# One kernel, three attentions: scores as 32x64 products in two halves, the x transposes between them, and the context groups of the gate stage ahead of the x groups

## The reference

```
x = x + tanh(g_xattn[0]) * cross_attention(layernorm(x), ctx, ctx)      # 16 heads of 8
x = x + tanh(g_ffn[0])   * two_transformer_layers(layernorm(x))         # below
x = x + tanh(g_xattn[1]) * mlstm_attention(layernorm(x), ctx, ctx)      # 8 heads of 16, gates
x = x + tanh(g_ffn[1])   * int8_linear(layernorm(x))
# each transformer layer, l = 0, 1:
for l in range(L):
    x = x + _attn(_ln(x, ln1_w[l], ln1_b[l]), wq[l], wk[l], wv[l], wo[l], ...)   # causal, 16 heads of 8
    h = _ln(x, ln2_w[l], ln2_b[l])
    x = x + moe(h, ...)                  # 8 experts, top 2; by token for l = 0, by sequence for l = 1
# the heart of each attention:
att = jnp.einsum('bhqd,bhkd->bhqk', q, k) * hd ** (-0.5)
att = jax.nn.softmax(jnp.where(causal, att, -jnp.inf), axis=-1)
y = jnp.einsum('bhqk,bhkd->bhqd', att, v)
```

## Time and profile before

| what | value |
|---|---|
| three runs | 1271.04, 1274.37, 1277.46 us, median 1274.37 |
| the profiled execution | 1265.2 us, its span 1263.5 us |
| TensorE (PE) busy | 980.7 us, 78% |
| VectorE (DVE) busy | 836.2 us, 66% |
| ScalarE (ACT) busy | 700.8 us, 55% |
| GpSimd (POOL) busy | 584.5 us, 46% |
| masked keys, L632 | 192 instructions, 240.9 us |
| scores, 64x512 | 768 records, 103.4 us |
| chain that ended last | PE 48%, DVE 12%, ACT 9%, POOL 7% |

### The profile page before, as it was taken

One profiled execution on the slowest core, in us unless ns is written; L12 is line 12 of the kernel. 1 busy time (PEld: TensorE's weight loads), 2 busy tenths in 40 slices (PEclk: granted clock), 3 DMA queues, 4 the chain that ended last, 5 costly groups with the idle time before them and its releaser, 6 DMA issues.

```text
span 1263.5 us, 30781 instructions
## 1 busy us (share of the span) xinstructions
PE 980.7 (78%) x9835; PEld 759.3 (60%) x9835; DVE 836.2 (66%) x1984; ACT 700.8 (55%) x1780; POOL 584.5 (46%) x804
## 2 busy tenths in 40 slices
PE   4999998999974899993005999965999978899503
PEld 2677676677674799993003777744777758555301
DVE  4599998999848566661425999976222245389874
ACT  2577677878730177772004777743555522588643
POOL 6355544655620255554773666612333310378423
PEclk9899999999965599997556999966999995699855
DMA  4000040000020022221214000000000001011102
GB/s 124 12 13 15 15 137 2 2 0 0 1 67 0 17 67 64 65 65 47 53 52 134 2 0 0 1 2 0 0 0 0 0 25 50 7 47 44 30 0 67
DMA packets 51918, 38.74 MB, mean 31 GB/s; under 512 B 6072, under 2 KB 45476, under 8 KB 51860
## 3 DMA queue, kind: packets, MB, share of 16 engines
q1 hardware_dynamic: 46956, 28.88, 7.8%
q0 software_dynamic: 4320, 8.86, 2.7%
q10 hardware_dynamic: 584, 0.26, 0.1%
HBM read 29.13 MB, written 8.85 MB: 30 GB/s over the span
## 4 chain that ended last, share of the span: by engine, by line
PE 48%; DVE 12%; issue 11%; ACT 9%; POOL 7%; POOLq 7%; DVEq 3%; DMA 2%; SPq 1%; ACTq 0%
PE ps_s L1000 9%; PE ps_o L1000 8%; PE ps_t L1084 7%; PE ps_v L1000 6%; PE ps_a L1000 5%; PE ps_t L1000 5%; POOLq L688 5%; POOL h_all L659 2%; POOL w L659 2%; ACT work L811 2%; POOL work L689 2%; DVEq L1599 2%; PE ps_v L1104 1%; POOLq L678 1%; PE ps_x L1039 1%
## 5 line engine op out<-in xcount | busy, mean ns | idle before, releaser
L632 POOL TENSOR_TENSOR kbd<-kts,kmask 128x512 f32<-128x512 f32 x192 | 240.9, 1276 | 223.1 <-ACT qts L797 140.8
L652 POOL DMA_INDIRECT xg<-x_rows,row_from x71 | 73.5, 1036 | 137.8 <-DVE slot_of L1592 70.1
L819 ACT COPY probs_t<-ps_t 128x1024 f32<-128x1024 f32 x96 | 97.2, 1012 | 68.4 <-PE ps_t L1084 68.4
L1427 DVE TENSOR_REDUCE rowmax<-ps_s 128x16 f32<-128x1024 f32 x96 | 116.5, 1213 | 17.0 <-PE ps_s L1000 16.9
L1000 PE MATMUL ps_s<-kbd,qts 64*64 64x512 f32 (+1 forms) x1024 | 124.6, 559 | 0.2 <-issue 0.2
L1430 DVE TENSOR_TENSOR work<-ps_s,rowmax 128x1024 f32<-128x1024 f32 x96 | 117.6, 1225 | 3.3
L1000 PE MATMUL ps_o<-vst,probs_t 128*64 128x18 f32 x3072 | 108.5, 214 | 5.3 <-ACT probs_t L819 5.3
L1000 PEld LDWEIGHTS ps_o<-vst,probs_t 128*64 128x64 f32 x3072 | 98.9, 139 | 17.6 <-ACT probs_t L819 6.9
L1039 PE MATMUL ps_x<-ident,xn 128*128 128x128 f32 x96 | 31.1, 323 | 100.8 <-DVE xn L1418 100.8
L1084 PE MATMUL ps_t<-ident,work 128*128 128x128 f32 x768 | 103.5, 279 | 7.2 <-ACT work L811 5.7
L811 ACT ACTIVATE work<-work 128x1024 f32<-128x1024 f32 x96 | 100.9, 1051 | 1.3 <-DVE work L1430 1.2
(11 more groups left out here) (370 smaller groups left out, 2382.2 us busy)
## 6 DMA issues: line engine op xcount, KB each, us to landing
y_rows<-work SPq DMA_DIRECT2D x71, 64.0 KB, 1.6
w<-in_L_ffn_e_w_dram SPq DMA_DIRECT2D x2, 2048.0 KB, 8.6
ctx_dup<-in_ctx_dram SPq DMA_DIRECT2D x64, 64.0 KB, 2.3
x_res<-in_x_dram SPq DMA_DIRECT2D x4, 512.0 KB, 6.6
ctx_in<-in_ctx_dram SPq DMA_DIRECT2D x32, 64.0 KB, 1.8
x_rows<-h_all SPq DMA_DIRECT2D x1, 2048.0 KB, 9.2
work<-in_ctx_dram SPq DMA_DIRECT2D x8, 256.0 KB, 2.7
out_dram<-work SPq DMA_DIRECT2D x16, 128.0 KB, 1.8
```

Source lines behind the costliest of these rows:

```text
L632: i = pool.tensor_tensor(km[:, par, g, :, :], kts[:, par, g:g + 1, :].to_broadcast([P, 8, SEQ]), kmask[:, :, :], ALU.mult)
L652: pool.indirect_dma_start(xg[:, t % XBUFS, :], None, x_d, bass.IndirectOffsetOnAxis(row_from[:, t:t + 1], 0)).then_inc(xg_loaded[t % XBUFS ...
L819: nc.scalar.copy(probs_t[:, par, :], ps_t[:, :]).then_inc(S["pts_ready"], 1)
L1427: V.tensor_reduce(rowmax[:, par, :], s3, AXX, ALU.max).then_inc(S["max_ready"], 1)
```

## The change

- The head mask `kmask` covers 4 heads (`HPG`) in place of 8, and repeats every 32 partitions. GpSimd makes the masked keys of both sequences in one instruction of half the elements.
- The scores of a tile are eight products in place of four, each over 32 partitions (4 heads) and 256 columns: a 32x64 part of the array. They are issued in two halves. In the first, groups 0, 1, 2, 3 of heads belong to sequences 0, 1, 0, 1; in the second, to 1, 0, 1, 0. Different rows of the array would write the same bank and partitions if the halves overlapped, so the second waits for the first (`half_scored`).
- TensorE's transposes of context and x stand between the halves, in place of after the v projection; they wait for ScalarE's copy of the tile before.
- The causal mask is two products of 64x128 parts (`ident_seqs` stacks an identity for each sequence), in place of four of 64x64.
- VectorE's `norm_step` has lag 0 in place of 1 and stands last in the turn.
- In the gate stage all 8 context groups, their copies and their gate products come before the first x group, on TensorE and on ScalarE; there `row_std` stands after the context copies.

```
+GROUPS = 4
+HPG = HEADS // GROUPS
...
-                    for g in range(SPT):
-                        i = pool.tensor_tensor(km[:, par, g, :, :],
-                                               kts[:, par, g:g + 1, :].to_broadcast([P, 8, SEQ]),
-                                               kmask[:, :, :], ALU.mult)
-                    i.then_inc(S["kbd_ready"], 1)
+                    pool.tensor_tensor(km[:, par, :, :, :],
+                                       kts[:, par, :, :].unsqueeze(2).to_broadcast([P, SPT, HPG, SEQ]),
+                                       kmask[:, :, :].unsqueeze(1).to_broadcast([P, SPT, HPG, SEQ]), ALU.mult
+                                       ).then_inc(S["kbd_ready"], 1)
...
-            row_std(CH_MLSTM)
             for g in range(NB):
                 act.wait_ge(S["cg_tr"], g + 1)
                 nc.scalar.copy(inner[:, g * BLK:(g + 1) * BLK], (ps_o, ps_v)[g % 2][:, :]).then_inc(S["cg_sb"], 1)
+            row_std(CH_MLSTM)
+            for g in range(NB):
                 act.wait_ge(S["xg_tr"], g + 1)
...
+            def score_products(t, par, turned, masked):
+                for u in range(GROUPS):
+                    q, r, at = (u + turned) % SPT, u // 2, u % 2 * HPG * SEQ
+                    h_ = slice(32 * u, 32 * u + 32)
+                    yield mm(ps_s3[64 * q:64 * q + 64, r, at:at + HPG * SEQ], qts[h_, par, q * SEQ:(q + 1) * SEQ],
+                             km[h_, par, q, :, :].rearrange("p h k -> p (h k)"), not masked, True)
...
-                    for s in range(SPT if masked else 0):
-                        for r in range(2):
-                            h_ = slice(64 * r, 64 * r + 64)
-                            mm(ps_s3[64 * s:64 * s + 64, r, :], identb[h_, h_],
-                               causal[h_, :, :].rearrange("p a b -> p (a b)"), True, False)
-                    for s in range(SPT):
-                        for r in range(2):
-                            h_ = slice(64 * r, 64 * r + 64)
-                            i = mm(ps_s3[64 * s:64 * s + 64, r, :], qts[h_, par, s * SEQ:(s + 1) * SEQ],
-                                   km[h_, par, s, :, :].rearrange("p h k -> p (h k)"), not masked, True)
+                    for r in range(2 if masked else 0):
+                        h_ = slice(64 * r, 64 * r + 64)
+                        mm(ps_s3[:, r, :], ident_seqs[h_, :, :].rearrange("p s q -> p (s q)"),
+                           causal[h_, :, :].rearrange("p a b -> p (a b)"), True, False)
+                    for i in score_products(t, par, 0, masked):
+                        i.then_inc(S["half_scored"], 1)
+                return fn
+
+            def other_scores(base, masked):
+                def fn(t, par):
+                    pe.wait_ge(S["half_scored"], GROUPS * (ATT[base] + t + 1))
+                    pe.sem_inc(S["scores_begun"], 1)
+                    for i in score_products(t, par, 1, masked):
+                        pass
                     i.then_inc(S["scores_ready"], 1)
...
                 return [(L_SCORES, scores(base, l is not None)),
+                        (1, ctx_transpose(base)) if l is None else None, (1, transposes(base, nbase)),
+                        (L_SCORES, other_scores(base, l is not None)),
                         (L_OUT, transpose_y(base)), (L_WEIGH, transpose_probs(base)),
-                        (2, project(base, l)), (1, ctx_transpose(base)) if l is None else None,
-                        (1, transposes(base, nbase)), (L_OUT, out_project(base, l)), (L_WEIGH, weigh(base), VBUFS)]
+                        (2, project(base, l)), (L_OUT, out_project(base, l)), (L_WEIGH, weigh(base), VBUFS)]
...
             for g in range(NB + 1):
                 if g < NB:
                     context_group(g)
+                if g:
+                    context_gates(g - 1)
+            for g in range(NB + 1):
+                if g < NB:
                     x_group(g)
                 if g:
-                    i = gates_group(g - 1)
+                    i = x_gates(g - 1)
...
-                return [(L_OUT, y_step(base)), (1, norm_step(src, nbase, base, norm)),
-                        (L_SCORES, shift_step(base)), (L_OUT + 1, sums_step(dst, "x_updated", UPD[base])),
-                        (L_OUT, add_step(base, dst, scale))]
+                return [(L_OUT, y_step(base)), (L_SCORES, shift_step(base)),
+                        (L_OUT + 1, sums_step(dst, "x_updated", UPD[base])), (L_OUT, add_step(base, dst, scale)),
+                        (0, norm_step(src, nbase, base, norm))]
```

More of the change, by code:

```diff
@@ L194, in build @@
         identb = sb("identb", [P, P], BF16)
+        ident_seqs = sb("ident_seqs", [P, SPT, SEQ], BF16)
         ones_row = sb("ones_row", [1, P])
@@ L197, in build @@
         ones_b = sb("ones_b", [P, P], BF16)
-        kmask = sb("kmask", [P, 8, SEQ])
+        kmask = sb("kmask", [P, HPG, SEQ])
         kmask4 = sb("kmask4", [P, 4, SEQ])
@@ L234, in build @@
         kts = sb("kts", [P, 2, SPT, SEQ])
-        kbd = sb("kbd", [P, 2, 8, P])
-        km = kbd[:, :, :, :].rearrange("p b a n -> p b (a n)").rearrange("p b (s h k) -> p b s h k", s=SPT, h=8)
+        kbd = sb("kbd", [P, 2, HPG, P])
+        km = kbd[:, :, :, :].rearrange("p b a n -> p b (a n)").rearrange("p b (s h k) -> p b s h k", s=SPT, h=HPG)
         vst = sb("vst", [P, VBUFS, SPT, HEADS // 2, 2, HD + 1])
@@ L250, in build @@
         ctx4 = work[:, 2 * BLK:4 * BLK].rearrange("p (b a d) -> p b a d", b=2, a=SUB)
-        km16 = kbd[:, :, 0:4, :].rearrange("p b a n -> p b (a n)").rearrange("p b (s h k) -> p b s h k", s=SPT, h=4)
+        km16 = kbd[:, :, :, :].rearrange("p b a n -> p b (a n)").rearrange("p b (s h k) -> p b s h k", s=SPT, h=4)
         txs = work[:, 6 * DFF:6 * DFF + 2 * TURN].rearrange("p (b n) -> p b n", b=2)
@@ L559, in _ @@
             CONSTS.append(n[0])
-            head_mask(kmask, KM_HEADS, HD, SEQ, KM_HEADS * HD)
+            head_mask(kmask, HPG, HD, SEQ, HPG * HD)
             def routing_constants():
@@ L564, in routing_constants @@
                 select(identb[:, :], [[-1, P]], 0, 1, ALU.not_equal, 1.0)
+                fresh(pool.memset(ident_seqs[:, :, :], 0.0))
+                for half in range(2):
+                    part = ident_seqs[half * 64:(half + 1) * 64, :, :]
+                    select(part, [[0, SPT], [-1, SEQ]], 0, 1, ALU.not_equal, 1.0)
                 fresh(pool.memset(causal[:, :, :], 0.0))
@@ L1027, in fn @@
                 def fn(t, par):
+                    seen(pe, S["xts_ready"], TB[base] + t)
                     pe.wait_ge(ctx_loaded[par], arrived(t, par, 16))
@@ L1038, in fn @@
                     pe.wait_ge(S["xn_ready"], nbase + t + 1)
+                    if base != "x":
+                        pe.wait_ge(S["xts_ready"], TB[base] + t)
                     nc.tensor.transpose(ps_x[:, 0:P], xn[:, par, :], ident[:, :]).then_inc(S["xt_ready"], 1)
@@ L1264, in x_group, with context_gates, x_gates @@
                 i.then_inc(S["xg_tr"], 1)
-            def gates_group(g):
+            def context_gates(g):
                 pe.wait_ge(S["cg_sb"], g + 1)
+                for t in range(g * SUB, (g + 1) * SUB):
+                    mm(ps_t[:, t * 16:(t + 1) * 16], tile(inner, t), wg_t[:, 1, :], False, False)
+            def x_gates(g):
                 pe.wait_ge(S["xg_sb"], g + 1)
                 for t in range(g * SUB, (g + 1) * SUB):
-                    mm(ps_t[:, t * 16:(t + 1) * 16], tile(inner, t), wg_t[:, 1, :], False, False)
                     i = mm(ps_t[:, t * 16:(t + 1) * 16], tile(h_t, t), wg_t[:, 0, :], False, True)
```

3 lines of the change are left out of this document (1 added, 2 removed).

## The result

The changed kernel takes 1298.36 us (median of four runs, 1297.45 to 1299.16), the kernel before 1273.34 (four runs, 1271.04 to 1277.46). The ratio is 1.0193, with a 95% interval of 1.0164 to 1.0222: slower, by 25 us. The forecast was 1296. The profiled execution took 1297.6 us, its span is 1295.9.

The account below looks back on a forecast made before the run. TensorE's unbroken work was taken to bound the loops, ScalarE's chain the first self-attention. Loops +32, gate stage -8, start -2 gave +22: 1287 us profiled, plus 9.2 to the median, 1296; stated range 1271 to 1317.

Parts of the forecast that it names:

- The bound of the loops: Attention loops: TensorE's own sum sets the turns at 4.62 and 4.68 us; ScalarE's chain sets the first self-attention's 4.96.
- Rival 2: Loops: VectorE, 97% busy, sets the pace; relieving it brings up to 60 us, 1214; 0.13 together with Rival 1.
- The price of a switch: Loops on TensorE: each change of tile shape costs 0.10 us in draining and 0.05 in starting.
- Rival 1: Loops: switches with 32-row tiles and the mask's are free or hidden; -10 us, 1264; 0.13 together with Rival 2.
- Rival 4: Scores: the four tiles of a set run two by two; +82 us, 1378; chance 0.04.
- Rival 5: Switches cost half (+16), gate stage gains 12, start 2: about no change, 1276 us; chance 0.08.
- The cross attention's rest: The 28 cross-attention turns after tile 3's probabilities: +8.7 us, at +0.31 a turn.
- The self-attentions: Self-attention loops: turns of 5.18 us in the first (+0.22) and 5.15 in the second (+0.47).
- its completion comes about 0.66 + 0.07 after A began ... cover of over 0.1 us: Loops: the second score set's wait for the first set (A) is hidden by the x transposes, at no cost.
- Rival 3: Loops: the x transpose waits for the normalise step, 0.2 us a turn; +19 us, 1315; chance 0.10.
- The gate stage: Stage after the second mixture of experts: new order gains 8 us, with 2 us idle and 4 saved by the clock.
- The start: Start-up: the normalise step of tile 1 no longer stands behind a cast awaiting late weights; -2 us (0 to -3).

Follow-up runs that it names:

- run 2: The kernel before with only VectorE's normalise step moved (lag 0, last in its turn); ratio 1.0018, no difference.
- run 4: The kernel before with each 64x64 score product cut in two, context and x transposes between the halves, normalise step a turn earlier; 1295.56 us, ratio 1.0165.
- run 5: The kernel before with the causal mask alone changed to two 64x128 products; 1281.53 us in a single execution.
- run 6: The kernel before with the gate stage's new order and two shape switches fewer a turn (q, k, v products behind the output product); 1233.9 us, ratio 0.9668.
- run 3: The changed kernel with context and x transposes put back behind the v projection, so the score halves follow each other; 1307.4 us, ratio 1.025.
- run 1: The kernel before with the gate stage's new order alone; 1265.21 us, ratio 0.9926.
- run 8: The kernel before with ScalarE's order alone changed: copies of q, k and v at the start of the next turn; 1258.74 us, ratio 0.9929.
- run 9: The changed kernel with GpSimd's masked keys as two instructions a turn, one per sequence; 1296.32 us in a single execution.
- run 10: The kernel of run 6 with GpSimd's masked keys of a turn as one full-size instruction in place of two; 1236.83 us, ratio 0.9701.

## Why the prediction was right, and where it was not

- **The bound of the loops** was right: TensorE's unbroken starts, not GpSimd's or VectorE's busy time. GpSimd lost half its keys and the time rose. Rival 2 deserved more than I gave it in one place: in the second self-attention VectorE was level with TensorE (run 2). That relieving it alone would not have paid follows from TensorE's unbroken starts; no run tries it.
- **The price of a switch** was right. The Trainium skill (TensorEngine Tiling (Array Packing), Key Properties) has TensorE drain when the mode changes; run 4 has it for 64x64 tiles with +0.36 for two switches, run 5 with +0.14 for one, run 6 with -0.25 for two removed. Rivals 1, 4 and 5 fell with the sets at 0.59 and the turn at 4.97. The cross attention's rest came out at +8.6 for 8.7, in part by luck: its turn grew by 0.35 and not by 0.31, and one long turn near the seam took 0.9 back (6.92 before, 6.05 after).
- **The self-attentions** were under-sized: "Second self-attention: all of it counts, 4.68 + 0.47 = 5.15" was 5.25. Two terms failed. The output product I put at 0.37 takes 0.42: with like shapes on both sides it holds 0.23 (run 6), with a switch behind it 0.32, with one on either side 0.42, so its start costs 0.10 and not the 0.05 of a transpose. And "its completion comes about 0.66 + 0.07 after A began ... cover of over 0.1 us" is wrong: it counts at 0.92 (run 3), so the second set waits 0.06 a turn. These made 18.3 of the forecast 14.6, together with the first turn, which takes 6.32 in place of 4.60; TensorE's clock is at the lower level there until 713.8. In the first the same excess was made good at the seam, whose turns of 7.40, 6.29 and 6.78 became 6.45, 5.26 and 6.43.
- **Rival 3** (the x transpose waits for the normalise step) did not come: the step ends at 105.20 in the cross attention, the x transpose starts at 105.36 there. It ends 0.09 after GpSimd's keys, as forecast.
- **The gate stage** gave 6.0 for 8. TensorE's idle time was 1.9 us (2 assumed); "4 us saved by the clock, as before" was the term that failed: 40.2 us of work and 1.9 idle took 40.3, so 1.8 was saved. The "as before" was chance: of the five profiles with the old order only two have the stretch that saved it (run 1).
- **The start** failed in sign: -2 was forecast, and with the turns' own growth tile 3 should have come 1.1 earlier; it came 1.7 later. The first probabilities are late, at 37.9 in place of 33.3: the set-up transposes, which go with the x transposes, now part the halves of tile 0, of which the second began at 30.01, 3.99 after the first. Run 3 puts them back and is there at 34.1, and yet at tile 3 only at 57.7. What I had left out is TensorE's clock. Its row from 34 to 42 and the transposes of the probabilities, first in before and then in run 3:

```profile
34.00:42.00 8.00, 8.00 (x62) 4.91 (x61) 1.06 (x4) 3.48 (x8) 2.50 (x2) 0.51 0.04 10
...
41.87 1.91 PE L1084 MATMUL ps_t<-ident,work 128*128 128x128 f32 x8
```

```profile
34.00:42.00 8.00, 7.90 (x64) 6.00 (x64) 2.64 (x5) 3.52 (x9) 1.26 (x1) 1.00 0.03 8
...
43.98 1.92 PE L1106 MATMUL ps_t<-ident,work 128*128 128x128 f32 x8
...
50.96 1.04 PE L1106 MATMUL ps_t<-ident,work 128*128 128x128 f32 x8
```

From the first probabilities to tile 3 run 2 takes 16.8 us, all at the upper level; before takes 21.4, with 10.2 of them at the lower; run 3 takes 23.6, with 12.1; after 18.6, with 3.5. So the step's early start is worth 0.8 by itself (the first probabilities at 32.5 in place of 33.3) and the other 4.6 of run 2 go with the clock. With the halves the clock rises late in all five profiles that have them (41.0 to 48.4, with 64x64 tiles too); what in their order keeps it low isn't isolated.

So the sum (+22 for the 25 of the medians) is close in part by luck: terms of either sign were off by 2 to 4, and the -4.3 of the second mixture of experts, which I had at nothing, made up for the second self-attention. Of the 9.2 us between the profiled execution and the median that I carried over, 6.5 can be the row fetch and 3.2 the clock in the gate stage.

## What to carry to other kernels

On a TensorE that runs without a gap, count the changes of tile shape in a turn before anything else: each is worth 0.12 to 0.18 us here (runs 4, 5 and 6). The version that puts like shapes side by side is 3.3% faster, of which the gate stage's order is 0.7% (run 1), ScalarE's order 0.7% (run 8) and the start some 4 us, where halving GpSimd's work gave the loops nothing. At the start, read the clock from the lengths of like products, and not from its row alone. Before moving a group, ask which wait it covers: the x transposes covered ScalarE's copy where they stood, and the wait for a half where they went. Two engines that are both gapless are both the bound, whatever the chain says.

## What the hardware showed that I had not expected

- TensorE sees its own result 0.26 us after the modelled end of the last product (0.92 after the first start of a 0.66 set).
- The combine after the row fetches has two paces. In each of the nine long executions VectorE starts some operations of a group 1.37 to 1.41 us apart (677.80, 679.19), in the three short ones never more than 0.43. The cause stays open.
- How many instructions GpSimd's loops issue changes the pace of a later stage: 148.6 and 153.0 us (after and run 9), 148.7 and 153.0 (runs 10 and 6), two pairs of kernels that differ in that alone. Idle time that the profile calls issue, before GpSimd's copies of rows there, is 65.3 and 65.2 us with one instruction (after, run 10), 66.9 and 68.7 (runs 9 and 6) with two. That it is where GpSimd's code lies is a guess that was not tried.
